# Attention denominators: four of six even key blocks are added on VectorE instead of summed one by one on TensorE

## The chip, the cores and the metric

One Trainium2 chip, one of its cores. The metric is the device time of one execution in microseconds (us), and lower is better. The core has TensorE (PE; its weight loads are listed as PEld), VectorE (DVE), ScalarE (ACT), GpSimd (POOL), SyncE (SP, which here only issues transfers) and DMA queues. Each engine works through its own instructions in program order, and the engines wait for each other through semaphores.

## The reference, cut to what matters

Two layers on 2048 tokens of width 256, each an attention-like part and a mixture of eight experts. The change lies in the attention of the second layer, between the layer norm of x (2048 queries) and `ctx_2048` (1601 keys and values, 8 heads of 32):

```
x = x + tanh(g_xattn[0]) * depool(layernorm(x), ctx_2048)
x = x + tanh(g_ffn[0])   * experts_top1(layernorm(x))
# second layer
logits  = einsum('bhqd,bhkd->bhqk', Q * 32**-0.5, K) + b        # plus the mask
weights = softmax(logits, axis=-1)                              # exp(l - max) / sum of exp
x = x + tanh(g_xattn[1]) * einsum('bhqk,bhkd->bhqd', weights, V)
# router of the second layer: rw1 is 256 x 1024
logits  = silu(layernorm(x) @ rw1 + rb1) @ rw2 + rb2
x = x + tanh(g_ffn[1]) * experts_top2(layernorm(x), logits)
```

## The kernel before, in words

The program is written out by hand, with one semaphore for each kind of event. Nothing is scheduled by a tool: what stands first in an engine's list runs first.

The attention runs in 8 **rounds** n. A round takes 512 queries and one half of the heads (4 of 8). The 1601 keys are cut into NK = 13 blocks kc of 128. A **step** is one pair (round, block). In each step:

- TensorE forms the scores of 4 heads (`scores`, L588, four matmuls of 512 columns into three PSUM banks in turn). ScalarE takes their exponent (L1286) into one of 16 buffers `PT` in SBUF, 128x512 each, so the ring holds four blocks.
- TensorE multiplies the exponents of the block before with the values (`values`, L603). Each head fills a quarter of the array, and each product is two passes, so a block is 8 matmul records.
- The denominator is the sum of all exponents. TensorE forms it with a matrix of ones (`summed`, L593), again 8 records for a group of four heads. Blocks 2, 4, 6, 8, 10 and 12 are summed directly. Blocks 0 and 1, 3, 5, 7, 9, 11 are first added up by GpSimd (L1445 for the first pair, L1448 for the others) in the buffer `ACC`, which TensorE sums at the end of the round. That makes seven groups a round.
- Beside this, the row maxima of the **next** round are prepared (`maxima`): 64 score matmuls of 402 columns (L570) into three PSUM banks in turn. VectorE reduces each (L1042), and with that the bank is free for the third matmul after it. TensorE's list has one such matmul after each of the four score matmuls of a step and one or two behind them (steps 0 to 11; 5, 5, 6, 5, 5, 6 and so on; none in step 12). After each 16 of them VectorE forms the split maximum (L1028 to L1030). GpSimd also prepares queries (L1400 to L1404).
- Parts 0 to 7 of `into_x` put the round before into X on VectorE, in steps 2 to 4 (L1064, L1068, L1073, and the statistics L693 in odd rounds).

Round 7 has no maxima to prepare. In it VectorE forms the normalised rows for the second router (`normed`, L1098), splits what TensorE has turned (`grouped`, L1108 and L1109) and splits the router weights (`router_weights`, L1115 and L1116, in steps 4 and 5). The weights `RW1` (1 MB) are loaded before the attention begins.

`interleaved` writes this order for all engines alike: in each step, four times `scores(n, kc, hh)` and one piece of `maxima`, then the pieces that are left, then `values` of the block before. VectorE's own `scores` is empty before the change:

```
interleaved(maxima, lambda *a: None, lambda *a: None, lambda n: None, lambda n: None, into_x, prepared)
```

Of the kernel before, what the change touches and what calls it, by code (L numbers as in the profile page):

```python
# [15 lines left out]
P = 128  # L16
# [60 lines left out]
def build(nc, cst, x, ctx_2048, plen, kmask, g_xattn, g_ffn, W_in, b_in, g_res, g_init, rw0, rb0, w01, w02,  # L77
          att_b, rw1, rb1, rw2, rb2, w11, w12, b12, out):
    es = ExitStack()
    with es:  # L80
# [5 lines left out]
        def sb(name, shape, dt=F32):  # L86
            at = taken[0]
            taken[0] += (shape[1] + 7) // 8 * 8
            assert taken[0] <= cols, taken[0]
            return placed(name, shape, at, dt)  # L90
# [18 lines left out]
        KS = sb("KS", [P, E * NK * P], F32R).rearrange("p (h k) -> p h k", h=E)  # L109
        V = sb("V", [P, NK * D]).rearrange("p (c d) -> p c d", d=D)  # L110
        QF = [sb(f"QS{i}", [P, 2048], F32R) for i in range(2)]
        QS = [v.rearrange("p (h q) -> p h q", h=4) for v in QF]
        AK = [sb(f"AK{i}", [P, 1024], F32R).rearrange("p (h c) -> p h c", h=8) for i in range(2)]
        AF = [sb(f"AU{i}", [P, 512], F32R) for i in range(2)]
# [73 lines left out]
        def w2_half(s, raw=False):  # L188
# [3 lines left out]

        RW1 = Z0[:, 0:2048].rearrange("p (k n) -> p k n", k=2)
        QT = [Z0[:, 2048 + 128 * i:2176 + 128 * i] for i in range(2)]
# [21 lines left out]
        d_x = [sem(f"d_x{g}") for g in range(4)]  # L216
        d_zero = [sem("d_zero0"), sem("d_zero1")]
        d_dep = [sem(f"d_dep{i}") for i in range(2)]
# [19 lines left out]
            [sem(f"{n}{l}") for l in range(2)] for n in ("v_la", "a_ex", "v_oh", "t_rank", "v_slot", "t_tab", "v_tab", "v_eid"))  # L238
        v_flag, t_flag, v_mbh, v_ka, t_ka = (sem(n) for n in ("v_flag", "t_flag", "v_mbh", "v_ka", "t_ka"))

# [7 lines left out]
            sem(n) for n in ("v_x2", "v_qn", "p_q", "t_q", "a_q", "t_pc", "v_pc", "v_m", "t_m", "a_m"))  # L248
        t_s, a_p, p_acc, t_v, a_ot, a_rec, t_rec, v_rt, t_ot, v_ot, v_x3 = (
            sem(n) for n in ("t_s", "a_p", "p_acc", "t_v", "a_ot", "a_rec", "t_rec", "v_rt", "t_ot", "v_ot", "v_x3"))  # L250

# [22 lines left out]
        def val_done(n, kc, hh):  # L274
            before = 80 * n + 4 * kc + 4 * max(0, (kc - 1) // 2)
            return before + hh + (5 if kc and kc % 2 == 0 else 1)

# [3 lines left out]
        def on_pool(kc):  # L281
            return kc == 0 or kc % 2 == 1

        def interleaved(maxima, scores, values, attended, turned_out, into_x, prepared):
# [38 lines left out]
        def _(e):  # L323
# [272 lines left out]
            def values(n, kc):  # L596
                hf = n % 2
                g = 52 * n + 4 * kc
                e.wait_ge(a_p, g + 4)
                if kc == 0 and n:  # L600
                    e.wait_ge(a_ot, n)
                for hh in range(4):
                    e.matmul(PB[6][32 * hh:32 * hh + 32, :], V[:, kc, (4 * hf + hh) * 32:(4 * hf + hh) * 32 + 32],  # L603
                             PT[(g + hh) % 16], start=kc == 0, stop=kc == NK - 1,
                             tile_position=(0, 32 * hh)).then_inc(t_v, 1)
                if not on_pool(kc):
                    if kc == 2 and n:
                        e.wait_ge(v_rt, n)
                    summed(n, kc, kc == 2, False, lambda hh: PT[(g + hh) % 16])
                if kc == NK - 1:  # L610
                    e.wait_ge(p_acc, acc_done(n, NK - 2, 3))
                    summed(n, kc, False, True, lambda hh: ACC[n % 2][:, 512 * hh:512 * hh + 512])
# [78 lines left out]
        def _(e):  # L691
# [409 lines left out]
            def grouped(c):  # L1101
                e.wait_ge(t_xr, c + 1)
                if c == 0:
                    e.wait_ge(t_s, 364)
                    e.wait_ge(t_v, 560)
                turned = PB[bank_of["xr", c]][:, 0:D].rearrange("p (k q) -> p k q", k=2)
                high, low = (v[c // 4][:, :, c % 4 * P:c % 4 * P + P] for v in (XGH, XGL))
                vc.step(e, e.tensor_copy(high, turned))  # L1108
                e.tensor_tensor(low, turned, high.bitcast(F32), ALU.subtract).then_inc(v_xg, 1)  # L1109
# [17 lines left out]

            interleaved(maxima, lambda *a: None, lambda *a: None, lambda n: None, lambda n: None, into_x, prepared)

# [3 lines left out]
            inv_std(12, NC)  # L1133
            e.wait_ge(t_v, 640)
            def partial(g):
# [18 lines left out]
        def _(e):  # L1154
# [4 lines left out]
            e.wait_ge(p_set, 1)  # L1159
            for l, buf in ((0, xn0), (1, xn1)):  # L1160
                e.dma_start(buf[0:P, :], zero).then_inc(d_zero[l], 16)

# [114 lines left out]
            def scores(n, kc, hh):  # L1277
                g = 52 * n + 4 * kc + hh
                e.wait_ge(t_s, g + 1)
                if g >= 16:  # L1280
                    m, rest = divmod(g - 16, 52)
                    k, h = divmod(rest, 4)
                    e.wait_ge(t_v, val_done(m, k, h))
                    if on_pool(k):
                        e.wait_ge(p_acc, acc_done(m, k, h))
                e.activation(PT[g % 16], PB[g % 3], ACT.Exp).then_inc(a_p, 1)  # L1286

            def attended(n):
                e.wait_ge(t_v, 80 * n + 80)
                if n:  # L1290
                    e.wait_ge(v_x3, n)
                e.activation(OT, PB[6], ACT.Copy).then_inc(a_ot, 1)
                e.activation(REC, PB[7], ACT.Copy).then_inc(a_rec, 1)
# [27 lines left out]
        def _(e):  # L1321
# [28 lines left out]
            def experts(l, nt, xn, into, **add):  # L1350
# [13 lines left out]
                e.wait_ge(v_tab[l], 1)  # L1364
                for z in d_zero:
                    e.wait_ge(z, 16)
                for i in range(4):
# [66 lines left out]
            def scores(n, kc, hh):  # L1434
                if n == 7 and kc == 1 and hh == 0:
                    power(rst[:, 0:12], 10)
                if not on_pool(kc) or kc == 0:
                    return
                g = 52 * n + 4 * kc + hh
                acc = ACC[n % 2][:, 512 * hh:512 * hh + 512]  # L1440
                e.wait_ge(a_p, g + 1)
                if kc == 1:
                    if n >= 2:
                        e.wait_ge(t_v, 80 * (n - 1))
                    e.tensor_tensor(acc, PT[(g - 4) % 16], PT[g % 16], ALU.add).then_inc(p_acc, 1)  # L1445
                else:
                    e.wait_ge(p_acc, acc_done(n, kc - 2, hh))
                    e.tensor_tensor(acc, acc, PT[g % 16], ALU.add).then_inc(p_acc, 1)  # L1448
# [13 lines left out]
        def _(e):  # L1462
# [98 lines left out]
            e.wait_ge(t_down[0], 2 * NT0)  # L1561
            e.dma_start(RW1, rw1.rearrange("(k p) n -> p k n", p=P)).then_inc(d_rw1, 16)
            e.dma_start(RW2, rw2.rearrange("(f p) n -> p f n", p=P)).then_inc(d_rw2, 16)
# [12 lines left out]
            for g in range(3):  # L1576
                finished(g)
            stored(0, 12)
            e.wait_ge(t_v, 640)

# [65 lines left out]
```

## Time and profile before

| | |
|---|---|
| time, 3 runs | median 1243.98 us (1239.08 to 1245.86) |
| profiled execution | 1242.3 us, its span 1240.5 us |
| granted TensorE clock, mean | 0.94 |
| attention, from the first scores to the last sum | about 413 to 856 us |
| one round of those 1 to 5 | 55.5 to 56.2 us |

The span is what the trace covers. All times inside the trace are counted from its start. The trace lists an instruction with its duration. Instructions that follow each other on one engine overlap a little, so the distance from start to start is the better price of one more.

### The profile page before, as it was taken

The page shows a single profiled execution, that of the slowest core. Times are in us where ns is not written, and L with a number is a line of the kernel's source. Part 1 is how long each engine was busy: PE and PEld are TensorE (multiplying, and loading weights), DVE is VectorE, ACT ScalarE, POOL GpSimd, SP SyncE. Part 2 cuts the span into 40 slices and gives each one's busy share as a digit, 9 for nine tenths or more (in the row PEclk, how much of TensorE's full clock was granted, in tenths as well). Part 3 has the DMA queues.
Part 4 walks back from the last instruction along what each step waited for, and adds up shares of the span by engine and source line. Part 5 has one row for each costly group of instructions (what it writes and reads, how often), then busy time and mean ns, then how long its engine had stood idle before and what let it go on. Part 6 is the DMA issues. An engine that isn't in the chain of part 4 may idle for free.

```text
span 1240.5 us, 20677 instructions
## 1 busy us (share of the span) xinstructions
PE 1097.6 (88%) x7126; PEld 828.5 (67%) x7126; DVE 789.7 (64%) x1815; ACT 524.3 (42%) x1129; POOL 522.6 (42%) x515
## 2 busy tenths in 40 slices
PE   4865999999968799999999999999953999999995
PEld 3665999999955444545545454535732999999994
DVE  5765767666659886766758676753147555565553
ACT  4111434443311355556555565565450333333331
POOL 1241111111104375756667575674263343434332
PEclk9956999999986899999999999999975999999998
DMA  6254877788831000000000000004341566666662
GB/s 223 72 170 170 323 308 291 305 320 332 339 139 69 1 1 1 1 18 1 1 1 18 1 2 18 1 31 139 121 136 51 159 178 210 181 204 203 181 208 58
DMA packets 51219, 160.71 MB, mean 130 GB/s; under 512 B 7435, under 2 KB 36493, under 8 KB 40109
## 3 DMA queue, kind: packets, MB, share of 16 engines
q1 hardware_dynamic: 38590, 138.42, 30.8%
q0 software_dynamic: 10464, 18.36, 5.7%
q10 hardware_dynamic: 2062, 2.60, 0.6%
q8 instruction: 60, 0.98, 0.3%
q14 instruction: 43, 0.34, 0.1%
HBM read 142.97 MB, written 16.38 MB: 128 GB/s over the span
## 4 chain that ended last, share of the span: by engine, by line
PE 67%; DMA 10%; DVE 10%; issue 6%; ACT 3%; POOL 2%; SPq 1%; DVEq 0%; ACTq 0%; POOLq 0%
PE PQ L457 20%; DMA out<-Z,SI 8%; PE PB L603 7%; PE PQ L588 7%; PE PB L570 5%; DVE Z L1042 4%; PE PB L593 4%; PE PB L503 3%; PE PB L333 3%; PE PB L484 3%; PE PQ L570 2%; PE PB L502 2%; PE PB L483 1%; PE PQ L644 1%; PE PQ L646 1%
## 5 line engine op out<-in xcount | busy, mean ns | idle before, releaser
L1042 DVE TENSOR_REDUCE Z<-PB 128x1 f32<-128x402 f32 x319 | 171.9, 566 | 72.0 <-PE PB L570 70.7
L588 PE MATMUL PQ<-QS,KS 128*128 128x512 f32 x416 | 173.6, 433 | 3.4 <-ACT Z L1286 2.0
L457 PE MATMUL PQ<-Z,WS 128*128 128x128 f32 x1472 | 173.8, 277 | 0.5 <-ACT Z L1198 0.5
L457 PEld LDWEIGHTS PQ<-Z,WS 128*128 128x128 f32 x1472 | 172.3, 194 | 2.2 <-ACT Z L1198 0.9
L1213 ACT ACTIVATE Z<-PQ,W 128x128 f32<-128x128 f32 x312 | 89.0, 368 | 162.7 <-PE PQ L457 162.7
L457 PEld LDWEIGHTS PQ<-Z,W 128*128 128x128 f32 x1248 | 152.6, 193 | 6.9 <-issue 3.0
L457 PE MATMUL PQ<-Z,W 128*128 128x128 f32 x1248 | 153.9, 277 | 2.6 <-issue 2.2
L588 PEld LDWEIGHTS PQ<-QS,KS 128*128 128x128 f32 x416 | 77.2, 189 | 101.7 <-issue 66.2
L1286 ACT ACTIVATE Z<-PQ 128x512 f32<-128x512 f32 x208 | 109.8, 603 | 81.7 <-PE PQ L588 81.6
L1286 ACT ACTIVATE WS<-PQ 128x512 f32<-128x512 f32 x208 | 109.7, 604 | 81.5 <-PE PQ L588 81.4
L570 PE MATMUL PB<-KS,QS 128*128 128x402 f32 x319 | 119.6, 385 | 15.6 <-DVE Z L1042 6.6
L1042 DVE TENSOR_REDUCE Z<-PQ 128x1 f32<-128x402 f32 x193 | 106.7, 566 | 36.3 <-PE PQ L570 35.5
L1361 POOL DMA_INDIRECT out<-Z,SI x39 | 62.7, 1607 | 158.0 <-DMA out<-Z,SI 134.1
L1448 POOL TENSOR_TENSOR WS<-WS,Z 128x512 f32<-128x512 f32 x80 | 104.5, 1334 | 38.8 <-ACT Z L1286 38.8
L1361 POOL DMA_INDIRECT yd<-Z,SI x23 | 22.7, 987 | 205.3 <-DVE Z L973 205.3
L570 PEld LDWEIGHTS PB<-KS,QS 128*128 128x128 f32 x319 | 62.0, 195 | 41.4 <-DVE Z L1042 27.2
L1354 POOL DMA_INDIRECT Z<-xn,SI x62 | 61.2, 988 | 60.9 <-issue 36.6
L570 PE MATMUL PQ<-KS,QS 128*128 128x402 f32 x193 | 74.8, 405 | 6.6 <-DVE Z L1068 2.4
L1223 ACT ACTIVATE QS<-WS 128x1024 fp32r<-128x1024 f32 x46 | 48.6, 1057 | 72.9 <-PE PB L503 56.1
L951 DVE CAST HP<-Z 128x256 fp32r<-128x256 f32 x78 | 25.5, 327 | 79.8 <-ACT Z L1213 79.8
L503 PE MATMUL PB<-QS,AU 128*128 128x512 f32 x184 | 69.6, 406 | 0.0
L484 PE MATMUL PB<-W2F,HP 128*128 (+1 forms) x156 | 61.0, 413 | 0.0
(306 smaller groups left out, 2101.9 us busy)
## 6 DMA issues: line engine op xcount, KB each, us to landing
WS<-in_w SPq DMA_DIRECT2D x23, 2048.0 KB, 7.9
W<-in_w SPq DMA_DIRECT2D x39, 1028.0 KB, 5.2
WS<-in_w SPq DMA_DIRECT2D x23, 1024.0 KB, 7.3
W2G<-in_w SPq DMA_DIRECT2D x8, 1024.0 KB, 9.4
xn<-WS SPq DMA_DIRECT2D x32, 128.0 KB, 1.8
X<-in_x SPq DMA_DIRECT2D x4, 512.0 KB, 11.7
WS<-yd SPq DMA_DIRECT2D x4, 512.0 KB, 5.5
out<-X SPq DMA_DIRECT2D x4, 512.0 KB, 2.8
```

The lines of the kernel that those rows point to most:

```text
L457: t = e.matmul(bank[:, j * P:j * P + P], w[:, k, o:o + P], FXT[i % 2][:, k * P:k * P + P], start=k == 0, stop=k == 1)
L484: t = e.matmul(PB[6 + i % 2], hh[:, j * P:j * P + P], both, start=first, stop=n == 1 and j == 3)
L503: t = e.matmul(PB[6 + i % 2], HA[:, j * P:j * P + P], W2P[n][:, j, :, :].rearrange("p s n -> p (s n)"), start=first, stop=last)
L570: e.matmul(PB[b][:, 0:PIECE], q[:, h, t4 * P:t4 * P + P], KS[:, 4 * hf + h, s * PIECE:(s + 1) * PIECE], start=True, stop=True).then_inc(t_ ...
L588: e.matmul(PB[g % 3], KS[:, 4 * (n % 2) + hh, kc * P:kc * P + P], QS[n % 2][:, hh, :], start=True, stop=True).then_inc(t_s, 1)
L603: e.matmul(PB[6][32 * hh:32 * hh + 32, :], V[:, kc, (4 * hf + hh) * 32:(4 * hf + hh) * 32 + 32], PT[(g + hh) % 16], start=kc == 0, stop=kc ...
L1042: e.tensor_reduce(MP[j % 2][:, i:i + 1], PB[bank_of["pc", r]][:, 0:PIECE], AX.X, ALU.max).then_inc(v_pc, 1)
L1213: t = e.activation(FS[c % 4][:, j * P:j * P + P], PB[c % 4][:, j * P:j * P + P], ACT.Silu, bias=W1[i % 2][:, o:o + 1])
L1286: e.activation(PT[g % 16], PB[g % 3], ACT.Exp).then_inc(a_p, 1)
L1354: e.indirect_dma_start(FXL[i % 4], None, xn, bass.IndirectOffsetOnAxis(ap=tabi[:, i:i + 1].bitcast(U32), axis=0)).then_inc(d_xl[l][i % 4], 16)
L1361: e.indirect_dma_start(into, bass.IndirectOffsetOnAxis(ap=tabi[:, i:i + 1].bitcast(U32), axis=0), FY[i % 2], None, **add).then_inc(d_y[l][ ...
L1448: e.tensor_tensor(acc, acc, PT[g % 16], ALU.add).then_inc(p_acc, 1)
```

## The change

- VectorE gets a `scores` of its own. In step 5 it adds the exponents of blocks 2 and 4 into a new buffer `ACCV` (four additions of 128x512, one for each head). In step 7 it adds block 6, and in step 9 block 8. Each addition stands ahead of one piece of `maxima`.
- TensorE sums directly only blocks 10 and 12, then `ACCV`, then `ACC`: four groups a round in place of seven.
- ScalarE waits for VectorE's addition, too, before it writes over a buffer of blocks 2, 4, 6 and 8.
- `ACCV` takes the place of `RW1`. `RW1` now lies over the query buffer `QS0`. So its load moves on SP's queue from ahead of the attention to the start of round 7 (after the 364th score matmul), and SP waits for the split weights before it writes over that place.
- The counts of the semaphore `t_v` follow (68 a round for 80). Two semaphores for zeroed rows become one.

```diff
-        RW1 = Z0[:, 0:2048].rearrange("p (k n) -> p k n", k=2)
+        ACCV = Z0[:, 0:2048]
...
+        RW1 = placed("RW1", [P, 2048], qs_at).rearrange("p (k n) -> p k n", k=2)
...
         def val_done(n, kc, hh):
-            before = 80 * n + 4 * kc + 4 * max(0, (kc - 1) // 2)
-            return before + hh + (5 if kc and kc % 2 == 0 else 1)
+            before = 68 * n + 4 * kc + (4 if kc > 10 else 0)
+            return before + hh + (5 if kc in (10, 12) else 1)
...
+        def vadd_done(n, kc, hh):
+            return 12 * n + 4 * (max(kc, 4) // 2 - 2) + hh + 1
+
+        def on_vector(kc):
+            return kc in (2, 4, 6, 8)
...
-                if not on_pool(kc):
-                    if kc == 2 and n:
+                if kc in (10, 12):
+                    if kc == 10 and n:
                         e.wait_ge(v_rt, n)
-                    summed(n, kc, kc == 2, False, lambda hh: PT[(g + hh) % 16])
+                    summed(n, kc, kc == 10, False, lambda hh: PT[(g + hh) % 16])
                 if kc == NK - 1:
+                    e.wait_ge(v_acc, vadd_done(n, 8, 3))
+                    summed(n, kc, False, False, lambda hh: ACCV[:, 512 * hh:512 * hh + 512])
                     e.wait_ge(p_acc, acc_done(n, NK - 2, 3))
                     summed(n, kc, False, True, lambda hh: ACC[n % 2][:, 512 * hh:512 * hh + 512])
...
-            interleaved(maxima, lambda *a: None, lambda *a: None, lambda n: None, lambda n: None, into_x, prepared)
+            def scores(n, kc, hh):
+                if kc - 1 not in (4, 6, 8):
+                    return
+                g = 52 * n + 4 * (kc - 1) + hh
+                acc = ACCV[:, 512 * hh:512 * hh + 512]
+                e.wait_ge(a_p, g + 1)
+                if kc - 1 == 4:
+                    if n:
+                        e.wait_ge(t_v, 68 * n)
+                    e.tensor_tensor(acc, PT[(g - 8) % 16], PT[g % 16], ALU.add).then_inc(v_acc, 1)
+                else:
+                    e.wait_ge(v_acc, vadd_done(n, kc - 3, hh))
+                    e.tensor_tensor(acc, acc, PT[g % 16], ALU.add).then_inc(v_acc, 1)
+
+            interleaved(maxima, scores, lambda *a: None, lambda n: None, lambda n: None, into_x, prepared)
...
+                    if on_vector(k):
+                        e.wait_ge(v_acc, vadd_done(m, k, h))
                 e.activation(PT[g % 16], PB[g % 3], ACT.Exp).then_inc(a_p, 1)
...
-            e.dma_start(RW1, rw1.rearrange("(k p) n -> p k n", p=P)).then_inc(d_rw1, 16)
             e.dma_start(RW2, rw2.rearrange("(f p) n -> p f n", p=P)).then_inc(d_rw2, 16)
...
+            e.wait_ge(t_s, 364)
+            e.dma_start(RW1, rw1.rearrange("(k p) n -> p k n", p=P)).then_inc(d_rw1, 16)
             stored(0, 12)
-            e.wait_ge(t_v, 640)
+            e.wait_ge(t_v, 544)
+            e.wait_ge(v_rw, 2)
```

VectorE's list in round 2, step 5, before the change: the reductions of the maxima (Z<-PB or PQ, L1042), then the split maximum (L1028 to L1030), then the first reductions of step 6.

```order
L1042 TENSOR_REDUCE Z_53<-PQ 128x1
L1042 TENSOR_REDUCE Z_53<-PB 128x1 x2
L1042 TENSOR_REDUCE Z_53<-PQ 128x1
L1042 TENSOR_REDUCE Z_53<-PB 128x1 x2
L1028 TENSOR_REDUCE Z_53<-Z_53 128x4
L1029 TENSOR_REDUCE AU_65<-Z_53 128x4
L1030 TENSOR_TENSOR AU_65<-Z_53,AU_65 128x4
L1042 TENSOR_REDUCE Z_53<-PQ 128x1
```

The same place of VectorE's list after the change (line numbers are ten higher; Z_53 holds `ACCV`, Z_54 and WS_56 hold exponents).

```order
L1147 TENSOR_TENSOR Z_53<-Z_54,WS_56 128x512
L1052 TENSOR_REDUCE Z_53<-PQ 128x1
L1147 TENSOR_TENSOR Z_53<-Z_54,WS_56 128x512
L1052 TENSOR_REDUCE Z_53<-PB 128x1
L1147 TENSOR_TENSOR Z_53<-Z_54,WS_56 128x512
L1052 TENSOR_REDUCE Z_53<-PB 128x1
L1147 TENSOR_TENSOR Z_53<-Z_54,WS_56 128x512
L1052 TENSOR_REDUCE Z_53<-PQ 128x1
L1052 TENSOR_REDUCE Z_53<-PB 128x1 x2
L1038 TENSOR_REDUCE Z_53<-Z_53 128x4
```

Four additions now stand between the reductions of the step, each ahead of one of them; nothing else moved there.

TensorE's list in round 3, from the middle of step 5, before the change: scores (L588), scores for the maxima (L570), the values of block 4 (L603), their sum (L593), and the start of step 6.

```order
L588 MATMUL PQ<-QS_61,KS 128x512
L570 MATMUL PB<-KS,QS_60 128x402 x2
L570 MATMUL PQ<-KS,QS_60 128x402
L603 MATMUL PB<-WS_56,V 32x512 x4
L593 MATMUL PB<-WS_56,CT 32x512 x4
L588 MATMUL PQ<-QS_61,KS 128x512
L570 MATMUL PB<-KS,QS_60 128x402
```

The same place of TensorE's list after the change.

```order
L596 MATMUL PQ<-QS_61,KS 128x512
L578 MATMUL PB<-KS,QS_60 128x402 x2
L578 MATMUL PQ<-KS,QS_60 128x402
L611 MATMUL PB<-WS_56,V 32x512 x4
L596 MATMUL PQ<-QS_61,KS 128x512
L578 MATMUL PB<-KS,QS_60 128x402
```

The sum of block 4 is gone from the end of step 5, and the scores of step 6 follow the values at once.

At the end of round 2 TensorE's list has, after the change, three groups one behind the other: block 12, `ACCV` (Z_53), `ACC` (WS_56). Before, it was the first and the last of them.

```order
L611 MATMUL PB<-WS_56,V 32x512 x4
L601 MATMUL PB<-WS_56,CT 32x512 x4
L601 MATMUL PB<-Z_53,CT 32x512 x4
L601 MATMUL PB<-WS_56,CT 32x512 x4
L596 MATMUL PQ<-QS_61,KS 128x512
```

The middle group is new and the other two are as before.

## Rows read from the trace of the kernel before

**Rows 1.** The page: busy time of each engine, share of the span, instructions

```profile
PE 1097.6 (88%) x7126; PEld 828.5 (67%) x7126; DVE 789.7 (64%) x1815; ACT 524.3 (42%) x1129; POOL 522.6 (42%) x515
```

**Rows 2.** Windows: from:to and length, busy time of each engine, granted clock; rounds 3 and 7

```profile
589.58:645.04 55.46, 53.54 (x321) 28.33 (x316) 38.10 (x79) 32.47 (x62) 37.53 (x40) 1.00 0.00 1
...
811.33:853.86 42.53, 38.99 (x241) 15.32 (x236) 23.53 (x41) 25.77 (x50) 32.22 (x24) 1.00 0.11 36
```

**Rows 3.** Windows by TensorE's steps 3, 5 and 12 of round 3; last, steps 5 to 10

```profile
601.28:605.34 4.06, 4.06 (x29) 2.00 (x25) 3.77 (x10) 2.07 (x4) 2.85 (x2) 1.00 0.00 0
...
609.38:613.94 4.56, 4.53 (x31) 2.19 (x27) 3.76 (x9) 2.07 (x4) 3.80 (x4) 1.00 0.00 0
...
638.07:641.29 3.22, 3.21 (x25) 1.72 (x21) 0.45 (x1) 2.60 (x5) 1.66 (x2) 1.00 0.00 0
...
609.38:633.51 24.13, 24.06 (x144) 12.83 (x140) 17.92 (x38) 14.12 (x27) 18.64 (x21) 1.00 0.00 1
```

**Rows 4.** Timeline, TensorE: start, duration; values, sums, and the scores behind them

```profile
603.49 1.06 PE L603 MATMUL PB<-Z,V 128*32 128x512 f32 x8
604.37 1.04 PE L593 MATMUL PB<-Z,CT 128*32 128x512 f32 x8
605.34 0.50 PE L588 MATMUL PQ<-QS,KS 128*128 128x512 f32 x1
...
644.86 1.90 PE L593 MATMUL PB<-WS,CT 128*32 128x512 f32 x16
646.69 0.50 PE L588 MATMUL PQ<-QS,KS 128*128 128x512 f32 x1
```

**Rows 5.** Timeline of VectorE and GpSimd in steps 3 to 5 of round 3

```profile
602.00 1.06 DVE L1042 TENSOR_REDUCE Z<-PB 128x1 f32<-128x402 f32 x2 [0.22 <-PE PB L570]
...
602.49 5.47 POOL L1448 TENSOR_TENSOR WS<-WS,WS 128x512 f32<-128x512 f32 x4 [2.51 <-ACT WS L1286]
...
602.97 1.35 DVE L1073 SCALAR_TENSOR_TENSOR X<-Z,SM,X 128x512 f32<-128x512 f32 x1
...
610.11 1.06 DVE L1042 TENSOR_REDUCE Z<-PB 128x1 f32<-128x402 f32 x2 [1.04 <-PE PB L570]
...
610.60 5.01 POOL L1448 TENSOR_TENSOR WS<-WS,Z 128x512 f32<-128x512 f32 x4 [0.72 <-ACT Z L1286]
```

**Rows 6.** By line: VectorE operations, shortest, median and longest duration in ns

```profile
L1042 DVE TENSOR_REDUCE Z<-PB x319: 511/566/577, 378.2 to 804.5; 128x1 f32<-128x402 f32 x160
...
L1073 DVE SCALAR_TENSOR_TENSOR X<-Z,SM,X x8: 742/1350/1354, 491.3 to 860.4; 128x512 f32<-128x512 f32 x8
...
L1030 DVE TENSOR_TENSOR AU<-Z,AU x32: 166/168/1187, 386.5 to 805.4; 128x4 fp32r<-128x4 f32 x32
...
L1013 DVE TENSOR_TENSOR X<-X,WS x16: 392/418/1371, 371.2 to 447.9; 128x256 f32<-128x256 f32 x16
```

**Rows 7.** Timeline, round 0: a late VectorE and the TensorE wait behind it

```profile
423.59 1.31 DVE L1013 TENSOR_TENSOR X<-X,WS 128x256 f32<-128x256 f32 x1
...
426.09 0.93 PE L570 MATMUL PB<-KS,QS 128*128 128x402 f32 x2 [1.68 <-DVE Z L1042]
```

**Rows 8.** Timeline of round 7: last scores of round 6, VectorE, GpSimd

```profile
808.65 1.69 PE L588 MATMUL PQ<-QS,KS 128*128 128x512 f32 x4
...
826.54 0.68 DVE L1115 CAST KS<-Z 128x1024 fp32r<-128x1024 f32 x1
...
831.50 2.18 DVE L1116 TENSOR_TENSOR KS<-Z,KS 128x1024 fp32r<-128x1024 f32 x1
...
841.30 5.04 POOL L1448 TENSOR_TENSOR WS<-WS,Z 128x512 f32<-128x512 f32 x4 [1.36 <-ACT Z L1286]
```

**Rows 9.** DMA issues: count, KB each, us from issue to landing

```profile
Z<-in_rw SPq DMA_DIRECT2D x1, 1024.0 KB, 9.0
```

**Rows 10.** Windows ahead of the rounds and in round 0: the granted clock is the third last number

```profile
402.00:408.00 6.00, 5.38 (x16) 3.28 (x15) 5.93 (x16) 0.59 (x1) 0.00 (x0) 0.72 0.00 0
...
420.00:426.00 6.00, 4.30 (x21) 1.91 (x20) 5.86 (x12) 3.75 (x7) 5.85 (x8) 1.00 0.00 0
```

More of the change, by code:

```diff
@@ L110, in build @@
         V = sb("V", [P, NK * D]).rearrange("p (c d) -> p c d", d=D)
+        qs_at = taken[0]
         QF = [sb(f"QS{i}", [P, 2048], F32R) for i in range(2)]
         QS = [v.rearrange("p (h q) -> p h q", h=4) for v in QF]
+        RW1 = placed("RW1", [P, 2048], qs_at).rearrange("p (k n) -> p k n", k=2)
         AK = [sb(f"AK{i}", [P, 1024], F32R).rearrange("p (h c) -> p h c", h=8) for i in range(2)]
@@ L216, in build @@
         d_x = [sem(f"d_x{g}") for g in range(4)]
-        d_zero = [sem("d_zero0"), sem("d_zero1")]
+        d_zero = sem("d_zero")
         d_dep = [sem(f"d_dep{i}") for i in range(2)]
@@ L238, in build @@
             [sem(f"{n}{l}") for l in range(2)] for n in ("v_la", "a_ex", "v_oh", "t_rank", "v_slot", "t_tab", "v_tab", "v_eid"))
-        v_flag, t_flag, v_mbh, v_ka, t_ka = (sem(n) for n in ("v_flag", "t_flag", "v_mbh", "v_ka", "t_ka"))
+        v_flag, t_flag, v_ka = (sem(n) for n in ("v_flag", "t_flag", "v_ka"))
         t_tr, a_tr, t_up, t_down, v_y = (
@@ L248, in build @@
             sem(n) for n in ("v_x2", "v_qn", "p_q", "t_q", "a_q", "t_pc", "v_pc", "v_m", "t_m", "a_m"))
-        t_s, a_p, p_acc, t_v, a_ot, a_rec, t_rec, v_rt, t_ot, v_ot, v_x3 = (
-            sem(n) for n in ("t_s", "a_p", "p_acc", "t_v", "a_ot", "a_rec", "t_rec", "v_rt", "t_ot", "v_ot", "v_x3"))
+        t_s, a_p, p_acc, v_acc, t_v, a_ot, a_rec, t_rec, v_rt, t_ot, v_ot, v_x3 = (
+            sem(n) for n in ("t_s", "a_p", "p_acc", "v_acc", "t_v", "a_ot", "a_rec", "t_rec", "v_rt", "t_ot", "v_ot", "v_x3"))
         t_xr, v_xr, v_xg, v_rw, t_hr, a_hr, t_lm, v_lt, t_lt = (
@@ L1104, in grouped @@
                     e.wait_ge(t_s, 364)
-                    e.wait_ge(t_v, 560)
+                    e.wait_ge(t_v, 476)
                 turned = PB[bank_of["xr", c]][:, 0:D].rearrange("p (k q) -> p k q", k=2)
@@ L1159, in _ @@
             e.wait_ge(p_set, 1)
-            for l, buf in ((0, xn0), (1, xn1)):
-                e.dma_start(buf[0:P, :], zero).then_inc(d_zero[l], 16)
+            for buf in (xn0, xn1):
+                e.dma_start(buf[0:P, :], zero).then_inc(d_zero, 16)
             trash = [WS[0][:, 0:D], WS[0][:, D:2 * D]]
@@ L1285, in scores @@
                         e.wait_ge(p_acc, acc_done(m, k, h))
+                    if on_vector(k):
+                        e.wait_ge(v_acc, vadd_done(m, k, h))
                 e.activation(PT[g % 16], PB[g % 3], ACT.Exp).then_inc(a_p, 1)
             def attended(n):
-                e.wait_ge(t_v, 80 * n + 80)
+                e.wait_ge(t_v, 68 * n + 68)
                 if n:
@@ L1364, in experts @@
                 e.wait_ge(v_tab[l], 1)
-                for z in d_zero:
-                    e.wait_ge(z, 16)
+                e.wait_ge(d_zero, 32)
                 for i in range(4):
@@ L1443, in scores @@
                     if n >= 2:
-                        e.wait_ge(t_v, 80 * (n - 1))
+                        e.wait_ge(t_v, 68 * (n - 1))
                     e.tensor_tensor(acc, PT[(g - 4) % 16], PT[g % 16], ALU.add).then_inc(p_acc, 1)
@@ L1577, in _ @@
                 finished(g)
+            e.wait_ge(t_s, 364)
+            e.dma_start(RW1, rw1.rearrange("(k p) n -> p k n", p=P)).then_inc(d_rw1, 16)
             stored(0, 12)
-            e.wait_ge(t_v, 640)
+            e.wait_ge(t_v, 544)
+            e.wait_ge(v_rw, 2)
             def last_rows():
```

## The prediction

> **What bounds the kernel now.** I read the page first. TensorE is busy 88% of the span and VectorE 64% [rows 1], but such shares mix stages, so I went to the windows of the stage that the change touches. A round of the attention takes 55.5 us, and in it TensorE is busy for 53.5 us, VectorE for 38.1 and GpSimd for 37.5 [rows 2]. TensorE sets the pace. Then I cut round 3 by TensorE's steps. In steps 5 to 10, where the new additions go, TensorE is busy for 24.06 of 24.13 us, VectorE for 17.92 and GpSimd for 18.64 [rows 3]. VectorE's slack is not spread evenly: in step 12 it works for 0.45 of 3.22 us [rows 3], and no addition is put there.
>
> TensorE and VectorE are tied. The maxima go through three banks, so TensorE can be at most three small matmuls ahead of VectorE's reductions. In round 0 the reader sees what a late VectorE does: an addition on it takes 1.31 us, and TensorE stands 1.68 us for a bank a little later [rows 7]. So in each stretch the slower of the two sets the time, and a gain on TensorE counts only while VectorE keeps up.
>
> **What TensorE saves.** Values start at 603.49 and the sum behind them at 604.37, so a group of eight takes 0.88 us. Two sums and the switch to the scores take 646.69 - 644.86 = 1.83 us and one takes 605.34 - 604.37 = 0.97, so a group more or less is 0.86 to 0.88 us [rows 4]. A round loses four groups (steps 3, 5, 7, 9) and gains one (in step 0 of the next): three groups, 2.6 us. Over 8 rounds that is 21 us, the whole gain if nothing else moved.
>
> **What VectorE's additions cost.** There are 12 a round, 96 in all, 128x512 with both inputs in SBUF. The nearest row is L1073, of the same size, with inputs and output in SBUF: 742 ns at the shortest, 1350 at the median of its 8 [rows 6]. Instructions in a row overlap by 0.08 (two reductions of 566 ns take 1.06 us, so one more costs 0.49) [rows 5, 6]. So an addition costs 0.66 us alone and 1.27 us in the long form.
>
> Which form holds here? The timeline shows what makes it long. At 602.97 L1073 begins while GpSimd is in its own four additions of exponents. It takes 1.35 us, and those four take 5.47 us where the next four take 5.01 [rows 5]. The tiny L1030, four elements wide, takes 166 ns mostly and up to 1187 [rows 6], and L1013 goes from 392 to 1371. The extra never passes the length of one GpSimd addition, 5.01 / 4 = 1.25 us. So a VectorE instruction with two SBUF inputs waits until GpSimd's instruction is over, and GpSimd's next waits for it in turn. A reduction from PSUM doesn't (511 to 577 ns over 319) [rows 6].
>
> The Trainium skill says the same and more sharply: on the page "SBUF — State Buffer", section "Who interferes with whom", a VectorE instruction with two SBUF inputs contends with a GpSimd one that reads SBUF, and one blocks the other in full. By that rule the long form is the price; without it the sum would go by 0.66 us. The trace agrees (742 against 1350 ns).
>
> And the new additions stand exactly there. In steps 5, 7 and 9 GpSimd adds blocks 5, 7 and 9; its first addition starts 610.60 - 609.38 = 1.2 us after the step [rows 3, 5]. VectorE's first addition of step 5 fits before that: VectorE idles 1.04 us at that place now [rows 5]. Then it has a reduction (0.49), meets GpSimd's first addition, waits, adds, reduces while GpSimd takes its next, waits about 1.25 - 0.49 = 0.76, and so on. One pair of addition and reduction costs about 1.25 + 0.66 = 1.9 us, not 1.15.
>
> **Steps 5 to 10 of a round, on VectorE.**
> - Now: 17.9 us of work [rows 3].
> - Twelve additions in the long form: 12 x 1.27 = 15.2, sum 33.1.
> - The first of each four comes before GpSimd's: 3 x 0.61 less, 31.3.
> - The first of step 5 fills idle time: 0.7 less, 30.6.
> Against 24.1 now this is +6.5 us. TensorE would need 24.1 - 3 x 0.88 = 21.5, so VectorE sets the pace.
> - Step 3 loses its sum, but VectorE has 3.77 us of work in its 4.06 [rows 3], so 0.3 of the 0.88 comes back.
> - Step 0 gains a group where VectorE has little to do: +0.9.
> That is +7.1 us a round, 50 us over rounds 0 to 6. Both ends: with a wait on nine additions of half of 0.61 instead, VectorE has 17.9 + 7.9 + 2.8 - 0.7 = 27.9, and a round costs +4.4, in all +31. With every addition in the long form and about 1 us lost in each pair of steps because the two engines then wait in turn, it has 36 us, a round costs +12.7, in all +89.
>
> **Round 7.** It takes 42.5 us for 13 steps, 3.3 each, with VectorE busy for 23.5 [rows 2]. No reductions stand between the four additions there, and GpSimd's four follow without a gap (5.04 us) [rows 8]. One run of four costs 0.66 + 3 x 1.9 = 6.4 us, and behind it stands the normalised row that TensorE turns a step later. That is 3.1 us more than a step, three times, and the router weights (2.18 us for one piece [rows 8]) stand behind the first run. VectorE's slack in the even steps gives some back. I take +8, with 0 and +12 as ends.
>
> **The router weights.** Their load took 9.0 us to land [rows 9]. Now it starts when the last scores of round 6 are done (808.65 + 1.69 = 810.3) and is first read at 826.54 [rows 8]: 16 us of cover, so nothing. Without cover it would cost at most 9. On SP's queue the load used to stand behind those that VectorE waits for ahead of the attention, so taking it out there gives nothing. SP's new wait for the split weights ends long before the attention does. The merged semaphore costs nothing: both zeroed rows landed in the first stage.
>
> ScalarE's new waits: the exponents of block 6 write over block 2's buffers, so they wait for the additions of step 5, which are one step earlier; late VectorE means late scores anyway. GpSimd has 18.6 us of work in those steps, and 12 blocks of 0.6 make it 26, less than the 30.6 they will take.
>
> **Sum.** 1242.3 + 50 + 8 = 1300.3 against the profiled execution's own time. That stands 1.7 us under the median of the runs, so I say 1300. The ends: 1242.3 + 31 + 0 = 1273 and 1242.3 + 89 + 12 = 1343.
>
> **The rivals.**
> 1. *The long form is rare.* Against it: at least half of the L1073 have it, as their median shows [rows 6]. VectorE has 17.9 + 7.9 - 0.7 = 25.1 us in steps 5 to 10, a little more than the 24.1 now. A round costs 1.0 - 0.3 + 0.9 = +1.6, seven 11. Round 7 gains up to its three groups, 2.6. This gives 1242.3 + 11 - 2.6 = 1251; with reductions that overlap better, 1245. Chance 0.12; it splits between no change and slower.
> 2. *It gets faster.* VectorE fits its additions into idle time and TensorE keeps its own pace, 21.5 us. The place is steps 5, 7 and 9. It needs an addition to cost no more than (21.5 - 17.9 + 0.7) / 12 = 0.36 us, and any gain in those steps needs less than (24.1 - 17.9 + 0.7) / 12 = 0.58. The shortest row says 0.66. At 0.36 the time is 1242 - 21 + the 4 us of step 3 = 1225. Chance 0.06.
> 3. *TensorE's clock falls too.* With VectorE slower, TensorE stands more. Ahead of the rounds, with TensorE fed only by reductions, the granted clock was 0.72, between its two levels of 1.2 and 2.4 GHz. In round 0, with VectorE just as late, but values and scores in between, it was 1.00 [rows 10]. Steps 5 to 10 will look like the second. If it fell to half for a part, the values would take 2 us for 1 at six places: up to +6 a round on top, 1300 + 42 = 1342. Chance 0.12.
>
> The forecast (each addition waits mostly for GpSimd's) has 0.70. Its own range is 1273 to 1325. The range for 8 in 10 takes in some of rival 1 and most of rival 3: 1258 to 1338. About 0.5% (6 us) is what a measurement of this kernel can tell from no change. Faster by more: 0.06. Within: 0.08. Slower: 0.86.
>
> **What would show it.** The additions' mean near 1.2 us with a shortest near 0.7; TensorE's small matmuls waiting for VectorE's reductions in steps 5, 7 and 9; rounds of 61 to 64 us; GpSimd's additions longer, near 1.5 us; the sum groups 32 a round in records for 56. I am wrong if the additions' mean is under 0.8 us, or if the rounds stay under 58 us though it is 1.2: then the two engines are tied less tightly than I think.

## The result

The changed kernel takes 1302.0 us (median of 4 runs, 1298.5 to 1306.9) against 1241.9 before (4 runs): a ratio of 1.049, 95% interval 1.045 to 1.052. The profiled execution took 1303.2 us, with a span of 1301.4.

The page after the change, to be read against [rows 1]: busy time, share of the span, instructions.

```profile
PE 1111.3 (85%) x6934; PEld 831.3 (64%) x6934; DVE 878.6 (68%) x1911; ACT 528.9 (41%) x1129; POOL 553.5 (43%) x515
```

VectorE works 89 us more, and TensorE 14 us more although it has 192 records fewer: some of what it has left ran at the lower clock (in round 7 the granted clock is 0.87 where it was 1.00).

Windows after the change, as [rows 2, 3]: rounds 1, 3 and 7, each from the first sum at a round's end to the next, then steps 5 and 6 of round 3 (step 6 up to TensorE's next values), then its steps 5 to 10.

```profile
487.52:548.96 61.44, 53.24 (x296) 27.31 (x292) 48.86 (x92) 32.79 (x62) 42.10 (x40) 1.00 0.00 1
612.19:673.65 61.46, 54.08 (x297) 28.55 (x292) 48.84 (x92) 33.06 (x62) 42.07 (x40) 0.97 0.00 1
...
862.78:915.00 52.22, 42.08 (x220) 16.16 (x216) 36.47 (x53) 26.23 (x51) 34.11 (x24) 0.87 0.11 38
...
632.72:638.31 5.59, 3.86 (x22) 1.93 (x18) 5.15 (x8) 2.07 (x4) 5.50 (x6) 0.98 0.00 0
638.31:642.79 4.48, 4.48 (x21) 2.87 (x17) 4.41 (x12) 2.40 (x4) 2.03 (x2) 0.65 0.01 2
...
632.72:662.30 29.58, 24.17 (x120) 13.14 (x116) 28.44 (x50) 14.56 (x27) 23.81 (x23) 0.94 0.00 1
```

In steps 5 to 10 VectorE is now busy for 28.44 of 29.58 us, where TensorE was for 24.06 of 24.13. In step 5 TensorE works 3.86 of 5.59 us.

Groups by form, each with its busy time and mean: the 96 additions.

```profile
L1150 DVE TENSOR_TENSOR Z<-Z,Z 128x512 f32<-128x512 f32 x32 | 36.5, 1148 | 0.0
L1150 DVE TENSOR_TENSOR Z<-Z,WS 128x512 f32<-128x512 f32 x32 | 32.0, 1008 | 0.0
L1147 DVE TENSOR_TENSOR Z<-Z,WS 128x512 f32<-128x512 f32 x16 | 20.0, 1264 | 0.0
L1147 DVE TENSOR_TENSOR Z<-WS,Z 128x512 f32<-128x512 f32 x16 | 17.0, 1060 | 0.0
```

Their mean is (36.5 + 32.0 + 20.0 + 17.0) / 96 = 1.10 us, and GpSimd's own additions grew beside them. By line: shortest, median and longest of one form, and from the page the mean of GpSimd's.

```profile
L1150 DVE TENSOR_TENSOR Z<-Z,WS x32: 672/977/1524, 455.5 to 902.0; 128x512 f32<-128x512 f32 x32
```

```profile
L1473 POOL TENSOR_TENSOR WS<-WS,Z 128x512 f32<-128x512 f32 x80 | 116.5, 1485 | 48.4 <-ACT Z L1312 48.4
```

The timeline of round 3, step 5: start, duration, and in brackets how long the engine stood and for whom. This is the place of the last two rows of [rows 5].

```profile
633.94 0.68 DVE L1147 TENSOR_TENSOR Z<-Z,WS 128x512 f32<-128x512 f32 x1
633.94 6.41 POOL L1473 TENSOR_TENSOR WS<-WS,Z 128x512 f32<-128x512 f32 x4
634.54 0.57 DVE L1052 TENSOR_REDUCE Z<-PB 128x1 f32<-128x402 f32 x1
635.02 1.28 DVE L1147 TENSOR_TENSOR Z<-Z,WS 128x512 f32<-128x512 f32 x1
635.16 0.45 PE L578 MATMUL PB<-KS,QS 128*128 128x402 f32 x1 [0.50 <-DVE Z L1052]
636.22 0.56 DVE L1052 TENSOR_REDUCE Z<-PQ 128x1 f32<-128x402 f32 x1
636.71 1.26 DVE L1147 TENSOR_TENSOR Z<-Z,WS 128x512 f32<-128x512 f32 x1
636.84 0.45 PE L578 MATMUL PQ<-KS,QS 128*128 128x402 f32 x1 [1.23 <-DVE Z L1052]
637.22 1.16 PE L611 MATMUL PB<-WS,V 128*32 128x512 f32 x8
```

The first additions are short (one at 632.33 too): GpSimd isn't adding yet or only starts. The two that fall well into its 6.41 us are long, one pair of addition and reduction takes 636.71 - 635.02 = 1.69 us, and each of TensorE's next small matmuls waits for a reduction. Over the kernel this is what grew. Of the view of one line's instructions, who waited for VectorE's reductions (us, times), before and after:

```profile
  PEld PB L570: 27.2, 68
  PE PB L570: 6.6, 8
```

```profile
  PEld PB L578: 63.7, 109
  PE PB L578: 32.9, 34
```

### The profile page after: what moved, and what is told of

The parts are those of the page before. It is cut to its first block, busy times and chain, and to the rows that moved or that the text cites. A ratio compares the mean times of both kernels' runs of the same rounds, so it can differ in the third digit from the quotient of the medians.

```text
span 1301.4 us, 20481 instructions
## 1 busy us (share of the span) xinstructions
PE 1111.3 (85%) x6934; PEld 831.3 (64%) x6934; DVE 878.6 (68%) x1911; ACT 528.9 (41%) x1129; POOL 553.5 (43%) x515
## 3 DMA queue, kind: packets, MB, share of 16 engines
q1 hardware_dynamic: 38590, 138.42, 29.4%
## 4 chain that ended last, share of the span: by engine, by line
PE 66%; DVE 19%; issue 7%; ACT 2%; DMA 2%; POOL 2%; SPq 1%; DVEq 0%; ACTq 0%; POOLq 0%
PE PQ L465 24%; DVE Z L1052 9%; PE PB L611 6%; PE PB L492 5%; PE PQ L596 4%; PE PB L578 3%; PE PB L511 3%; PE PB L341 3%; DVE Z L1150 3%; PE PB L491 2%; PE PB L601 2%; DVE Z L1147 2%; PE PQ L578 2%; PE PB L510 1%; PE PQ L654 1%
## 5 line engine op out<-in xcount | busy, mean ns | idle before, releaser
L596 PE MATMUL PQ<-QS,KS 128*128 128x512 f32 x416 | 181.2, 452 | 3.8 <-ACT Z L1312 2.6
L578 PE MATMUL PB<-KS,QS 128*128 128x402 f32 x319 | 126.7, 406 | 41.9 <-DVE Z L1052 32.9
L596 PEld LDWEIGHTS PQ<-QS,KS 128*128 128x128 f32 x416 | 81.3, 199 | 107.5 <-issue 69.7
L1473 POOL TENSOR_TENSOR WS<-WS,Z 128x512 f32<-128x512 f32 x80 | 116.5, 1485 | 48.4 <-ACT Z L1312 48.4
L578 PE MATMUL PQ<-KS,QS 128*128 128x402 f32 x193 | 78.7, 422 | 20.1 <-DVE Z L1052 15.4
L1380 POOL DMA_INDIRECT Z<-xn,SI x62 | 61.5, 992 | 60.9 <-issue 35.9
L961 DVE CAST HP<-Z 128x256 fp32r<-128x256 f32 x78 | 24.9, 320 | 81.2 <-ACT Z L1237 81.2
L1473 POOL TENSOR_TENSOR WS<-WS 128x512 f32<-128x512 f32 x40 | 57.2, 1459 | 31.1 <-ACT WS L1312 31.1
```

The costliest lines, as they stand in the source:

```text
L578: e.matmul(PB[b][:, 0:PIECE], q[:, h, t4 * P:t4 * P + P], KS[:, 4 * hf + h, s * PIECE:(s + 1) * PIECE], start=True, stop=True).then_inc(t_ ...
L596: e.matmul(PB[g % 3], KS[:, 4 * (n % 2) + hh, kc * P:kc * P + P], QS[n % 2][:, hh, :], start=True, stop=True).then_inc(t_s, 1)
L1380: e.indirect_dma_start(FXL[i % 4], None, xn, bass.IndirectOffsetOnAxis(ap=tabi[:, i:i + 1].bitcast(U32), axis=0)).then_inc(d_xl[l][i % 4], 16)
```

## The experiments

In the first four kernels the additions stay where they are, with every wait around them, but one engine's (or both engines') add one column of 512. That takes away their work and nothing of the order. "Waits" below are the time that an instruction of VectorE or GpSimd is longer because the other engine's is still running; they stand inside its duration.

**Which part is the work, and which the waits?** GpSimd's additions small, in the kernel after (`g_small_after`) and, as a control, before (`g_small_before`):

```diff
-                    e.tensor_tensor(acc, PT[(g - 4) % 16], PT[g % 16], ALU.add).then_inc(p_acc, 1)
+                    e.tensor_tensor(acc[:, 0:1], PT[(g - 4) % 16][:, 0:1], PT[g % 16][:, 0:1], ALU.add).then_inc(p_acc, 1)
```

The later additions are cut in the same way. The last sum reads the exponents of block 12 again in place of `ACC`, so most of the softmax's sum is left out.

> The changed kernel with GpSimd's additions of exponents cut to one column (the order and all waits stay; TensorE's last group reads the exponents of block 12 in place of the buffer that GpSimd would fill, so the denominators leave out blocks 0, 1 and the odd ones and count block 12 twice). My theory (the new additions are dear because they wait for GpSimd's): their mean falls from 1.10 us to about 0.70, rounds 0 to 6 to about 56 to 57 us, and the time to 1245 to 1258 us. Rival (it is VectorE's own extra work, whoever runs beside it): the time stays above 1285 us.

Measured: 1247.3 us, ratio 1.005 (1.002 to 1.007). By line, the same form of addition as above:

```profile
L1150 DVE TENSOR_TENSOR Z<-Z,WS x32: 674/682/752, 448.3 to 848.9; 128x512 f32<-128x512 f32 x32
```

> The kernel before with the same cut of GpSimd's additions (same part of the denominators left out): a control. Both theories: 1236 to 1244 us, no change that can be told, since TensorE sets the pace and VectorE waits for GpSimd only for some 1 us a round here.

Measured: 1236.0 us, ratio 0.996 (0.994 to 0.997). GpSimd's additions cost 5.9 us before the change (most of it in round 0; rounds 1 to 6 take the same within 0.1 us without them) and 54.7 after it. With them gone, all 64 additions of this line lie between 0.67 and 0.75 us. The long form is GpSimd's doing.

VectorE's additions small in the kernel after (`v_small`); the group of `ACCV` reads block 12's exponents:

```diff
-                    e.tensor_tensor(acc, acc, PT[g % 16], ALU.add).then_inc(v_acc, 1)
+                    e.tensor_tensor(acc[:, 0:1], acc[:, 0:1], PT[g % 16][:, 0:1], ALU.add).then_inc(v_acc, 1)
```

> The changed kernel with VectorE's new additions cut to one column (the denominators leave out blocks 2, 4, 6, 8 and count block 12 twice). The work is gone, but each still has two inputs in SBUF and still meets GpSimd's additions. My theory (a wait for GpSimd's instruction in flight): the tiny additions have a median or mean well above 0.17 us, about 0.5, and the time is 1235 to 1255 us, not the 1221 of TensorE's saving. Rival (the cost is work alone): mean near 0.17 us and 1218 to 1228 us.

Measured: 1247.9 us, ratio 1.006 (1.003 to 1.008). By line:

```profile
L1150 DVE TENSOR_TENSOR Z<-Z,Z x32: 141/207/1237, 460.8 to 844.3; 128x1 f32<-128x1 f32 x32
L1147 DVE TENSOR_TENSOR Z<-Z,WS x16: 145/454/1244, 557.3 to 837.6; 128x1 f32<-128x1 f32 x16
```

An addition of one column still takes up to 1.24 us, nearly the whole of one GpSimd addition (1.25). Even without its work, the wait eats the whole gain of the three groups.

Both small (`both_small`, the two edits together):

> Both cuts at once (denominators leave out all but blocks 10 and 12). Neither work nor waits of the additions are left, only TensorE's three groups fewer a round. Both theories: 1219 to 1230 us. If it stays near 1242, the groups that TensorE no longer does were not on the path at all, and my price of 0.88 us a group is wrong.

Measured: 1217.0 us, ratio 0.982 (0.978 to 0.986), 2 us below the expected range. By line, and a window of one round:

```profile
L1150 DVE TENSOR_TENSOR Z<-Z,Z x32: 147/149/158, 453.7 to 812.4; 128x1 f32<-128x1 f32 x32
```

```profile
578.49:631.55 53.06, 50.95 (x296) 27.47 (x292) 36.72 (x92) 32.47 (x62) 11.55 (x40) 1.00 0.00 1
```

Like has to be compared with like: GpSimd's additions are small here, so the new order alone is worth 1236.0 - 1217.0 = 19.0 us, for the 21 of the prediction. The rest of the 24.9 us under the kernel before is what GpSimd's additions cost there. To the 1217.0 come GpSimd's work and the waits on it, without VectorE's work (1247.9 - 1217.0 = 30.9, of which GpSimd's additions cost 5.9 before the change too), or VectorE's work without the waits (1247.3 - 1217.0 = 30.3). Both at once cost 85.0, 24 more than their sum.

Where the 24 us come from is only shown in part. The additions' own waits are longer when both engines do their full work: some 40 us in all (96 additions of 1.10 us in the mean for 0.68) against 30 (0.46 for 0.15). A second part may be common slack: VectorE's work in steps 5 to 10 is 17.9 us and TensorE's pace without the sums would be 21.5, 3.6 a round, and it hides either cost once but not both. By itself that would give 29 us over 8 rounds. The traces don't bear it out evenly: the excess is 1.7 to 3.7 us in each of rounds 1 to 6, 0.3 in round 0, and 6.8 in round 7, which has no reductions at all; another 3 us lie ahead of the attention, where runs differ by as much.

**Does another step help?** In `even`, blocks 6 and 8 are added one step later, where GpSimd's list has no additions:

```diff
-                if kc - 1 not in (4, 6, 8):
+                if kc not in (5, 8, 10):
                     return
+                kc = kc - 1 if kc > 5 else kc
```

> The changed kernel with the additions of blocks 6 and 8 one step later on VectorE (steps 8 and 10 in place of 7 and 9; blocks 2 and 4 stay in step 5). Same work, other neighbours: GpSimd starts its blocks in the odd steps and is idle for part of the even ones. My theory: fewer additions wait, their mean falls under 1.0 us, and the time falls by 5 to 25 us against 1302, to 1277 to 1297 us. Rival (only the amount of work on VectorE counts): 1302 +- 4 us.

Measured: 1300.8 us, ratio 1.049 (1.047 to 1.050). A miss. By form:

```profile
L1151 DVE TENSOR_TENSOR Z<-Z,Z 128x512 f32<-128x512 f32 x32 | 30.3, 955 | 0.0
L1151 DVE TENSOR_TENSOR Z<-Z,WS 128x512 f32<-128x512 f32 x32 | 27.1, 855 | 0.0
...
L1040 DVE TENSOR_TENSOR AU<-Z,AU 128x4 fp32r<-128x4 f32 x32 | 17.3, 541 | 1.1
```

The additions did get shorter (1148 and 1008 ns in the kernel after). But L1040, four elements wide, went from 385 to 541 ns: other instructions of VectorE now meet GpSimd more. From values to values, steps 5 to 10 of round 1 take 29.4 us for 29.6. Which of the later instructions takes the gain back was not isolated.

**How does the cost grow with the blocks?** In `two_four` only blocks 2 and 4 are added on VectorE, in step 5; TensorE sums 6, 8, 10 and 12, six groups a round:

```diff
-                if kc - 1 not in (4, 6, 8):
+                if kc != 5:
```

> A smaller dose: only blocks 2 and 4 are added on VectorE (four additions a round, in step 5), TensorE sums 6, 8, 10 and 12 directly: six groups a round in place of seven. Measured in the changed kernel, steps 5 and 6 of round 3 took 10.1 us against 7.8 before. My theory: +2.0 to +2.5 us in rounds 0 to 6 less nothing for the group saved there, +2 in round 7, in all 1254 to 1266 us. Rival (slower only once VectorE is full over the whole round, as with 12 additions): 1236 to 1243 us.

Measured: 1270.8 us, ratio 1.023 (1.022 to 1.025). My expectation was too low. With four additions a round in place of twelve, half of the loss stays. In the odd rounds the group saved in step 3 gives 0.3 us, step 5 and what follows it take 2.3 more, and the extra group at the round's end costs 0.85; rounds 2, 4 and 6 lose 3.4 to 4.1 us each, and round 7 loses 5.4.

**And in the idle step 12?** In `late`, blocks 10 and 12 are on VectorE, both in step 12, six groups on TensorE; the router weights are loaded as in the kernel after:

```diff
-                if kc - 1 not in (4, 6, 8):
+                if kc != 12:
```

> Another place: VectorE adds blocks 10 and 12 in step 12, where it has no maxima to reduce (0.45 of 3.22 us busy before) and GpSimd is mostly done; TensorE sums 2, 4, 6, 8 directly: six groups a round. Four additions a round as in the small dose. My theory: the saving of 0.88 us is kept in most rounds, 1235 to 1240 us. Rival (an addition on VectorE costs the same wherever it stands, by the waits at the end of the round): 1250 us or more.

Measured: 1239.9 us, ratio 0.999 (0.998 to 1.001), at the edge of what was expected, but no difference from before, so the saving was not kept. A round takes 55.47 us as before. The timeline of round 3 shows why the group that was saved at block 10 gives nothing:

```profile
635.04 5.51 POOL L1473 TENSOR_TENSOR WS<-WS,WS 128x512 f32<-128x512 f32 x4 [0.84 <-ACT WS L1312]
...
637.86 0.95 DVE L1040 TENSOR_TENSOR AU<-Z,AU 128x4 fp32r<-128x4 f32 x1
...
638.87 0.66 PE L341 MATMUL PQ<-CT,AU 128*128 128x128 f32 x4 [0.84 <-DVE AU L1040]
```

TensorE comes 0.84 us earlier to the transposition of the split maximum, and stands there until VectorE's L1040, itself behind GpSimd, has made it. Before the change VectorE's split ended just as TensorE got there, and there was no wait. The 0.88 us of the group turned into one.

In `late2` GpSimd adds block 8 as well, five groups (`ADDED` lists its blocks):

```diff
+        ADDED = (1, 3, 5, 7, 8, 9, 11)
-            return kc == 0 or kc % 2 == 1
+            return kc == 0 or kc in ADDED
```

> As the run before, and GpSimd adds block 8 as well (28 additions a round for 24; it has 18 us free in a round), so TensorE has five groups a round for seven. My theory: 1226 to 1236 us. Rival (GpSimd then ends too late for block 11, or VectorE meets it more often): 1240 us or more.

Measured: 1262.2 us, ratio 1.016 (1.014 to 1.018). A miss. The timeline of round 3 (GpSimd, VectorE, TensorE):

```profile
642.61 5.03 POOL L1475 TENSOR_TENSOR WS<-WS,Z 128x512 f32<-128x512 f32 x4
...
649.55 6.34 POOL L1475 TENSOR_TENSOR WS<-WS,WS 128x512 f32<-128x512 f32 x4
...
649.94 6.50 DVE L1149 TENSOR_TENSOR Z<-Z,WS 128x512 f32<-128x512 f32 x4 [0.67 <-ACT WS L1314]
...
656.98 0.45 PE L580 MATMUL PB<-KS,QS 128*128 128x402 f32 x1 [2.75 <-DVE Z L1054]
```

GpSimd's additions now run late, block 11's fall on the very ones that VectorE makes in step 12, the two take turns for 6.3 to 6.5 us, and the next round's reductions stand behind them on VectorE.

**Is TensorE off the path?** `sums_kept` is the kernel after, with TensorE summing blocks 2, 4, 6 and 8 directly too (they are counted twice, so this one's softmax is another):

```diff
-                if kc in (10, 12):
+                if not on_pool(kc):
```

> The changed kernel, but TensorE sums blocks 2, 4, 6 and 8 directly as well (32 more groups; those blocks count twice in the denominators). It has the cost of VectorE's additions without what they were to save. My theory (VectorE sets the pace in steps 5 to 10, so the groups taken away there had saved little): 1303 to 1318 us. Rival (the groups taken away were a full saving, and the additions cost about 81 us): 1302 + 32 x 0.88 = 1330 us.

Measured: 1310.1 us, ratio 1.056 (1.053 to 1.058). Four groups a round more, 32 x 0.88 = 28 us of TensorE's work, cost only 8 us. In those steps TensorE has time to spare, and a group saved there is worth under a third of itself. The clock has a part in the 8 us too: in step 6 of round 6 it was 1.00 here and 0.50 in the kernel after, and that round took 62.4 us here for 63.1, in spite of four groups more.

**The rest of the change.** `router_only` is the kernel before with only the move of `RW1`:

```diff
-            e.dma_start(RW1, rw1.rearrange("(k p) n -> p k n", p=P)).then_inc(d_rw1, 16)
...
+            e.wait_ge(t_s, 364)
+            e.dma_start(RW1, rw1.rearrange("(k p) n -> p k n", p=P)).then_inc(d_rw1, 16)
```

> The kernel before with nothing but the move of the router weights: their buffer over the query buffer, their load at the start of round 7, SP's wait for the split weights. My theory: nothing, 1239 to 1246 us. Rival (a late load or SP's wait costs part of the 9 us): 1247 to 1252 us.

Measured: 1241.3 us, ratio 1.001 (0.999 to 1.002). It costs nothing.

**GpSimd in VectorE's place.** The kernel before, with block 2 (`pool_two`) or blocks 2 and 6 (`pool_two_six`) added by GpSimd, which has 18 us of idle time a round:

```diff
+        ADDED = (1, 2, 3, 5, 7, 9, 11)
-            return kc == 0 or kc % 2 == 1
+            return kc == 0 or kc in ADDED
```

> The kernel before with block 2 added by GpSimd too (28 additions a round for 24), nothing on VectorE: six groups a round on TensorE. GpSimd has 18 us free in a round, but 8.8 of them ahead of its first addition. My theory (a group counts 0.86 us in the interval behind the values of block 2, and GpSimd catches up before the end): 7 us less, 1233 to 1238 us. Rival (GpSimd's later end holds TensorE's last group or VectorE's split maxima): 1240 us or more.

> As the run before, with block 6 on GpSimd as well (32 additions a round, 47.5 us of work in a round of 54 of which it stands for some 8 at the start). My theory: GpSimd is now late, and the saving of the second group is lost or more: 1236 to 1256 us. Rival (it still keeps up): 1226 to 1232 us.

Measured: 1238.5 us, ratio 0.999 (0.998 to 1.000), and 1242.3 us, ratio 1.002 (1.000 to 1.004). Windows of round 3 and round 7 of the first:

```profile
591.59:646.70 55.11, 53.14 (x312) 27.99 (x308) 37.75 (x80) 32.54 (x62) 42.43 (x44) 1.00 0.00 1
811.81:856.84 45.03, 39.77 (x237) 15.45 (x233) 27.28 (x41) 25.87 (x51) 38.51 (x28) 0.96 0.11 36
```

The first lies just outside the 1233 to 1238 us of its theory: a round gains 0.35 us of the group's 0.88, and round 7 takes 2.5 us more than in [rows 2]. With block 6 too, a round gains 1.3 us, but in round 6 TensorE once stands 5.7 us for a reduction of VectorE's. The trace shows what VectorE was late for, a split of four elements (it takes 0.17 us alone):

```profile
790.14 6.60 DVE L1032 TENSOR_TENSOR AU<-Z,AU 128x4 fp32r<-128x4 f32 x1
...
781.86 9.97 POOL L1450 TENSOR_TENSOR WS<-WS,Z 128x512 f32<-128x512 f32 x8
791.79 4.92 POOL L1450 TENSOR_TENSOR WS<-WS 128x512 f32<-128x512 f32 x4
```

GpSimd's additions of three blocks follow each other here without a gap, and the split ends with the last of them (796.7). It did not get in between two of them but stayed out for five in a row. No other VectorE instruction of the attention, in any of the traces, is over 1.3 us longer than the shortest of its kind. The 12 runs of this kernel spread from 1236.8 to 1248.7 us, and the profiled one is among the slow ones (1247.6). Why it happened here alone stays open. No version that does the whole work beats the kernel before by more than can be measured.

## Why the prediction was right

- **Its likeliest case held:** 1302.0 us for 1300. The attention, from its first score matmul to the end of its last sums, takes 501.0 us for 442.5. That is +58.4, and the prediction said 58. The profiled execution is 60.9 us longer in all: the attention starts 3.6 us later (its start lies between 412.8 and 416.9 us over all traces), and what follows it is 1.1 us shorter.
- **The long form.** An addition takes 1.10 us in the mean ("near 1.2"), and the shortest 0.67 ("near 0.7"). These are durations; less the overlap of 0.08, one costs 1.02, where the sum had nine of 1.27 and three of 0.66, 1.12 in the mean. GpSimd's take 1.49 ("near 1.5"). The Trainium skill's rule (page "SBUF — State Buffer", section "Who interferes with whom"), that a VectorE instruction with two SBUF inputs and a GpSimd one that reads SBUF block each other in full, agrees with the one-column addition of 1.24 us and with 0.67 to 0.75 us once GpSimd is nearly idle. One wait here was longer than a single GpSimd instruction, the 6.60 us in `pool_two_six`. The reductions from PSUM stay at 0.51 to 0.58.
- **Steps 5 to 10:** +6.5 said. From values to values it is +5.4 to +5.6 in rounds 1, 3 and 5, +6.6 in round 2, +7.8 and +8.0 in rounds 4 and 6, and +8.3 in round 0. The mean of rounds 1 to 6 is 6.5, and that is partly luck. In the odd rounds the sum was 1.1 us too dear: VectorE is busy for 28.4 us of the 30.6 said. In rounds 2, 4 and 6 come two things that the sum had not: the batch statistics (of the odd round before) fill the idle time in front of step 5's first addition, and the clock falls.
- **Step 3's group** gives 0.32 (0.3), and the extra group at the round's end costs 0.85 (0.9).
- **Rounds 0 to 6:** rounds 1 to 6 take 5.9 to 8.4 more, 41.8 in all, and round 0 with its lead-in 58.4 - 41.8 - 9.5 = 7.1: 48.9 for the 50 said. The upper end was added up a little high: 36.1 - 24.1 + 0.6 is 12.6 a round for the 12.7 written, and 1 us less in all.
- **Round 7:** +9.5 for +8. From values to values, the first run of four and the step behind it cost 5.8 us, the second 4.2, and the third nothing, where the prediction had 3.1 for each less some slack. The timeline shows the first run on VectorE, and the normalised row (L1108) behind it:

```profile
880.60 6.79 DVE L1147 TENSOR_TENSOR Z<-Z,WS 128x512 f32<-128x512 f32 x4
...
887.31 0.40 DVE L1108 TENSOR_SCALAR WS<-X,SM 128x256 f32<-128x256 f32 x1
...
887.77 0.69 PE L341 MATMUL PB<-CT,WS 128*128 128x128 f32 x2 [4.13 <-DVE WS L1108]
```

  It takes 6.79 us (6.4 said), and TensorE waits 4.13 for the row. The row itself has one tensor input, and it meets GpSimd too: the same line takes 0.40 to 1.37 us here, and 0.40 to 0.42 with GpSimd's additions small (`g_small_after`). The prediction had the long form for two inputs only.
- **The router weights** cost nothing, as said.
- **Rival 3, the clock,** was right in kind and too dear. In step 6 the granted clock falls in every round from 0 to 6 but round 1. In step 6 of round 3 it is 0.65, that is in part the lower of the two levels, after TensorE had worked 3.86 of 5.59 us. But round 3 takes 61.46 us and round 1, at a clock of 1.00 throughout, 61.44: there VectorE sets the pace and hides TensorE's lower clock. In the even rounds it doesn't. The same step of round 4, from values to values, in the kernel after and in `even`, whose lists are alike in that place:

```profile
700.69:706.24 5.55, 5.55 (x18) 3.02 (x18) 4.32 (x11) 2.36 (x4) 1.63 (x1) 0.50 0.00 0
```

```profile
700.08:704.17 4.09, 3.78 (x18) 1.61 (x17) 4.02 (x11) 2.12 (x4) 1.90 (x2) 1.00 0.01 2
```

  So by this comparison the clock costs about 1.5 us in round 4, as much in round 6 (5.55 too) and 0.5 in round 2 (4.56), not 6 a round. Round 7 ran at 0.87; what that cost was not separated.
- **Rival 2's** threshold (an addition below 0.58 us gains something in those steps) is bracketed: with GpSimd's additions small in both kernels, the change costs 11.3 us at 0.68 us an addition (1247.3 for 1236.0) and gains 19.0 at 0.15.
- **Where the size was off:** the sum worked with one time for VectorE in each stretch and took the effects one by one. The expectations of `even`, `two_four` and `late2`, made on that basis, missed. That of `two_four` left out the extra group at the round's end and took round 7 at 2 us for 5.4. In `even` and `late2` single instructions met GpSimd more than before (L1040, and the additions of step 12), and no sum over a stretch shows those.

## What to carry over

Before work moves from one engine to another, ask with which third engine it will have to take turns. In these traces the price of a VectorE instruction with two SBUF inputs was its own time plus what was left of GpSimd's instruction, however small it was itself (once it was five of GpSimd's in a row). A gain on the engine that sets the pace counts only as far as the next one's slack, here at most 3.6 us in a round's steps 5 to 10, and everything added there draws on the same slack, so costs that were measured one by one (31 and 30 us) need not add up (85). The cheapest test is to shrink the work to one column and leave the waits, for each engine and for both: it gave 19 us for the order, 31 for the waits and 30 for the work before any design was tried.

## What was not expected of the hardware

- An addition of 128x1 takes 0.15 us alone and up to 1.24 us beside GpSimd's 128x512 additions, so the wait doesn't shrink with the instruction that waits. A split of four elements on the path (0.17 us alone, 0.95 in step 12) cancelled a saved group of 0.88 us in `late`, and in `pool_two_six` one such split took 6.60 us, shut out by five of GpSimd's additions in a row.
- At a granted clock of 0.65 over a step in which TensorE was busy all the time (4.48 of 4.48 us), the round took no longer: 61.46 us for 61.44. In round 4 the same step at 0.50 took 5.55 us for 4.09 at 1.00.
- Four fewer groups a round were worth 8 us of their 28 in the kernel after, and one group fewer nothing that could be measured in `late` and in `pool_two`.
